# First stage of a fused cross-attention and feed-forward kernel: context loads one chunk ahead of x's, q's tanh one step later, a fourth PSUM bank

## The chip, the core and the metric

The kernel runs on one core of a Trainium2 chip. The metric is the device time of one execution in microseconds (us). Before the change it is 258.02 us, the median of three runs (257.67 to 258.16).

## The reference

The inputs `x` and `ctx_1024` are 128 x 64 x 128 in f32: 8192 rows of D = 128 features, in 128 batches of 64 rows. What is computed, cut to what matters:

```
q = layernorm(x)                      # no gain or bias
k = v = ctx
prob(t) = clip(p / (sum(p) + 1e-8), 1e-8), p = tanh(t)*0.499 + 0.5
sid  = (prob(q) - prob(k)) @ (log prob(q) - log prob(k)).T     # per batch, 64 x 64
attn = softmax(-sid / sqrt(D))
f    = (v - attn @ v) @ W_diff.T + b_diff + q
out  = layernorm(gelu(layernorm(f) @ W1.T + b1) @ W2.T + b2 + f)
x    = x + out
y    = x + (fp8(layernorm(x)) @ fp8(Wf).T + bf)
```

## The kernel before, in words

The 8192 rows are 64 tiles of 128 rows, taken in 16 chunks of G = 4 tiles. A chunk of x or of the context is 128 x 512 in f32, 256 KB. The kernel has three stages, each written as a step function that `run_steps` calls with a growing step number; `at(lag)` gives the chunk that entered `lag` steps ago. Each engine (SP for loads, POOL, ACT, DVE, PE) has its own program with its own order of work, and the engines meet only at counting semaphores. Nothing reorders the work: the order written by hand is the order in which an engine does it.

The first stage, which the change touches, prepares all 16 chunks. For chunk k:

- SP, in `load` (L305): loads the context chunk into one of two buffers `ctx_c` (L309), as soon as the tanh of the chunk two before it has ended and PE has transposed that chunk; then x's chunk (L312), once DVE has the variance of the chunk two before (L311). The waits hold up everything that is behind them on SP. Between the loads stand those of W1 (L316), W2 and small rows.
- ACT, in `phase1` (L520): at lag 0 four tanh of k, each with a sum (L525), and the copy of the transposed context out of PSUM (`vT_c`, L530); at lag 1 the copy of the product with W_diff out of PSUM (`PV`, L536); at lag 2 four tanh of q (L541). Once, eight steps in, it scales W1 (`W1h`, L547).
- PE, in `phase1` (L986): at lag 0 four transposes of the context (L992), at lag 1 four products with W_diff into one of three banks `P_B` (L1001), at lag 2 the bias row added by a matmul with a selector (L1010). The bank of chunk k is free when DVE has added the product of chunk k-3 (L999). At the step of `W_AT` = 6 it turns W1 and multiplies W2 (L1015, L1016).
- DVE, in `phase1` (L791): at lag 0 the statistics of x (L796) and, later in the step, the variance (L753 to L768); at lag 3 the sum of the product in PSUM and q into `F` (L801), which waits for q's tanh; at lag 1 the normalised q (L822), after POOL's power (L365). Two steps also copy the products of W1 and W2 (L804, L806), and one splits W1 (L810).
- After step 13 of lag 3, `take_norms` (L770, L777 to L787) turns the sums of 14 chunks into the gains that the second stage needs, and after the last step those of the last two chunks. Then the second stage begins, on DVE with L852.

The second stage (`phase2`) makes the differences and log ratios, the similarities, the softmax and the product with v. The third (`phase3`) runs the MLP, the two layer norms, the fp8 product and the stores.

Of the kernel before, what the change touches and what calls it, by code (L numbers as in the profile page):

```python
# [37 lines left out]
def wait(eng, sem, count):  # L38

    if count <= 0:  # L40
        return
    eng.wait_ge(sem, count)


def is_piece(k, n):

    return k.live and k.n == n
# [8 lines left out]
def xattn_ffn_kernel(nc, x, ctx_in, W_diff, b_diff, ln_g, ln_b, W1, b1, W2, b2, Wf, bf, out):  # L56
# [32 lines left out]
    out_d = out.rearrange("b s d -> (b s) d").rearrange("(t p) d -> p t d", p=P)  # L89

    EARLY = 2
    NORMS = NC - 2
    BF_HERE = NP - 3
    XQ_HERE = NP - 4
# [2 lines left out]
    with ExitStack() as ctx:  # L97
# [86 lines left out]
        centre = E_c[:, D:2 * D]  # L184
        sel_raw = E_c[:, 2 * D:3 * D]

        VT_B, P_B = (bank[0], bank[7]), (bank[1], bank[2], bank[6])
        D_B, L_B, S_B, EP_B = bank[2], bank[3], (bank[4], bank[7]), (bank[5], bank[6], bank[1])
        M1_B, M2_B, HT_B, XQ_B, FF_B = (bank[2], bank[3], bank[7]), (bank[4], bank[1]), bank[0], bank[5], bank[6]

# [111 lines left out]

        @block.sync
        def _(sp):
            def load(k):  # L305

                wait(sp, tanh_k, k.n - 1)
                wait(sp, vT_ps, k.n - 1)
                sp.dma_start(tiles(buf(ctx_c, k)), ctx_d[:, k.at:k.at + k.g]).then_inc(ctx_sem[k.buf], 16)  # L309

                wait(sp, x_var, k.n - 1)  # L311
                sp.dma_start(tiles(chunk(X, k)), x_d[:, k.at:k.at + k.g]).then_inc(x_in[k.buf], 16)  # L312

            for k in chunks[0:5]:
                load(k)
            sp.dma_start(W1_raw.rearrange("p (j d) -> p j d", d=D),  # L316
                         W1.rearrange("(j p) d -> p j d", p=P)).then_inc(w_in, 16)
            load(chunks[5])
            sp.dma_start(W2_raw, W2).then_inc(w_in, 16)
            load(chunks[6])  # L320
            sp.dma_start(g_col[:, :], ln_g.unsqueeze(1), allow_slow_non_contiguous=True).then_inc(w_in, 16)
            sp.dma_start(b_col[:, :], ln_b.unsqueeze(1), allow_slow_non_contiguous=True).then_inc(w_in, 16)
            sp.dma_start(b1_raw[:, :], b1.rearrange("(j p) -> p j", p=P),
                         allow_slow_non_contiguous=True).then_inc(w_in, 16)
            for k in chunks[7:]:
                load(k)
            for row, vec in ((b2_r, b2), (g_r, ln_g), (bf_r, bf)):
                sp.dma_start(row, vec.unsqueeze(0).broadcast_to([P, D])).then_inc(rows_in, 16)
            sp.wait_ge(bd_hl_ready, 1)
            sp.dma_start(Wf_raw, Wf).then_inc(wf_in, 16)  # L330

            def phase3(at):
                for k in last_of(at):
                    sp.wait_ge(y_ready, k.n + 1)
                    sp.dma_start(out_d[:, k.at:k.at + k.g], tiles(chunk(F, k))).then_inc(stored, 16)
                k = at(3)
                if k.live and k.n < XQ_HERE:
                    sp.wait_ge(xq16_ready, k.n + 1)
                    wait(sp, ff_ps, k.n - 1)
                    sp.dma_start_transpose(tiles(buf(xqT_c, k)), buf(xq16_c, k)).then_inc(xqT_in[k.buf], 16)  # L340

            run_steps(pieces, 4, phase3)
            sp.wait_ge(stored, 16 * NP)
# [168 lines left out]
        def _(act):  # L512
# [7 lines left out]
            def phase1(at):  # L520
                k = at(0)
                if k.live:
                    act.wait_ge(ctx_sem[k.buf], 16 * (k.n // 2 + 1))
                    for i in range(k.g):
                        last = act.activation(all_tile(TK, k, i), tile(ctx_c, k, i), ACT.Tanh,  # L525
                                              accum_out=per_tile(SUMK, k, i))
                    last.then_inc(tanh_k, 1)
                    act.wait_ge(vT_ps, k.n + 1)
                    wait(act, P_ps, k.n - 1)
                    act.activation(buf(vT_c, k), VT_B[k.buf][:, 0:k.g * D], ACT.Copy).then_inc(vT_sb, 1)  # L530
                k = at(1)
                if k.live:
                    act.wait_ge(P_ps, k.n + 1)
                    if is_piece(k, 0):
                        act.wait_ge(consts, CONSTS)
                    act.activation(pv_chunk(k), tiles(P_B[k.n % 3][:, 0:k.g * D]), ACT.Copy).then_inc(P_sb, 1)  # L536
                k = at(2)
                if k.live:
                    act.wait_ge(q_ready, k.n + 1)
                    for i in range(k.g):  # L540
                        last = act.activation(all_tile(TQ, k, i), all_tile(F, k, i), ACT.Tanh,  # L541
                                              accum_out=per_tile(SUMQ, k, i))
                    last.then_inc(tanh_q, 1)
                if is_piece(k, W_AT + 2):
                    act.wait_ge(w1u_sb, 1)
                    act.wait_ge(w_in, 16 * 5)
                    act.activation(W1h[:, :], W1u, ACT.Identity, scale=g_col[:, 0:1]).then_inc(w_sb, 1)  # L547

            run_steps(chunks, 2, phase1)

            act.preload_act_table_set("natural_log_exp_and_others")

# [163 lines left out]
        def _(dve):  # L716
# [72 lines left out]
                dve.wait_ge(norms, part + 1)  # L789

            def phase1(at):  # L791
                s, q, r = at(0), at(1), at(3)
                if s.live:
                    dve.wait_ge(x_in[s.buf], 16 * (s.n // 2 + 1))
                    for i in range(s.g):
                        last = dve.bn_stats(xstat[:, (s.buf * G + i) * 6:(s.buf * G + i + 1) * 6], all_tile(X, s, i))  # L796
                    last.then_inc(x_bn, 1)
                if r.live:
                    dve.wait_ge(tanh_q, r.n + 1)
                    dve.wait_ge(pb_ps, r.n + 1)  # L800
                    dve.tensor_tensor(chunk(F, r), P_B[r.n % 3][:, 0:r.g * D], chunk(F, r), ALU.add).then_inc(pq_ready, 1)  # L801
                if is_piece(r, W_AT):
                    dve.wait_ge(w_ps, 1)
                    dve.tensor_copy(W1u, bank[3][:, :]).then_inc(w1u_sb, 1)  # L804
                if is_piece(r, W_AT + 1):
                    dve.tensor_copy(W2T[:, :], bank[4][:, :]).then_inc(wt_sb, 1)  # L806
                if is_piece(q, NC - 1):

                    dve.wait_ge(w_sb, 1)
                    dve.scalar_tensor_tensor(out=W1l[:, :], in0=bank[3][:, :], scalar=g_col[:, 0:1],  # L810
                                             in1=W1h[:, :].bitcast(F32), op0=ALU.mult,
                                             op1=ALU.subtract).then_inc(w_done, 1)
                if s.live:
                    wait(dve, q_ready, s.n - 1)
                    stats_terms(s, x_bn, x_halves)
                    stats_halves(s, x_halves, x_terms)
                    stats_var(s, x_terms, x_var)
                if q.live:
                    dve.wait_ge(x_rstd, q.n + 1)
                    for i in range(q.g):  # L820
                        m = (q.buf * G + i) * 2
                        last = dve.tensor_scalar(all_tile(F, q, i), all_tile(X, q, i), xmv[:, m:m + 1],  # L822
                                                 xrstd[:, q.buf * G + i:q.buf * G + i + 1], ALU.subtract, ALU.mult)
                    last.then_inc(q_ready, 1)
                if is_piece(r, NORMS - 1):
                    take_norms(0, NORMS, 0)

                    dve.wait_ge(b1_ps, 1)
                    dve.tensor_tensor(b1c[:, :], bank[5][:, 0:HB], b1_raw[:, :], ALU.add).then_inc(b1_ready, 1)

            run_steps(chunks, 3, phase1)

            take_norms(NORMS, NC, 1)

# [145 lines left out]
        def _(pe):  # L980
# [5 lines left out]
            def phase1(at):  # L986
# [8 lines left out]
                if k.live:  # L995
                    if is_piece(k, 0):
                        pe.wait_ge(wd_sb, 1)
                    pe.wait_ge(vT_sb, k.n + 1)
                    wait(pe, pq_ready, k.n - 2)  # L999
                    for i in range(k.g):  # L1000
                        last = pe.matmul(P_B[k.n % 3][:, i * D:(i + 1) * D], tile(vT_c, k, i), WdT[:, :],  # L1001
                                         start=(i == 0), stop=False, skip_group_check=True)
                    last.then_inc(P_ps, 1)
                k = at(2)
                if k.live:
                    if is_piece(k, 0):
                        pe.wait_ge(bd_hl_ready, 1)
                        pe.wait_ge(sel_ready, 1)
                    pe.wait_ge(P_sb, k.n + 1)
                    pe.matmul(P_B[k.n % 3][:, 0:k.g * D], sel[:, :], over_tiles(bd_hl[:, :], k.g), start=False, stop=True,  # L1010
                              skip_group_check=True).then_inc(pb_ps, 1)
                if is_piece(k, W_AT):
                    pe.wait_ge(w_in, 16 * 5)
# [8 lines left out]

            pe.wait_ge(wt_sb, 1)
            for j in range(HB):
                last = pe.matmul(bank[5][:, j:j + 1], W1u[:, j * D:(j + 1) * D], b_col[:, :], start=True, stop=True)
            last.then_inc(b1_ps, 1)

            def turn_h(h):
# [148 lines left out]
```

## Time and profile before

| what | value |
|---|---|
| median of 3 runs | 258.02 us (257.67 to 258.16) |
| the profiled execution's own time | 258.79 us |
| its span in the profile | 256.9 us |
| busy: PE, DVE, ACT, POOL | 208.1, 222.6, 217.6, 190.3 us |
| first stage, to the start of its last `take_norms` | 64.5 us |
| mean granted TensorE clock | 0.937 of full |

The span is the time between the first and the last instruction that the profile shows; the execution's own time is 1.89 us more. Busy times say how full an engine was over the whole kernel, not which one set the end. For that the chain of waits is followed, and for a stage the timeline, where each instruction has its start, its duration and, in brackets, how long its engine had been idle and what released it.

### The profile page before, as it was taken

Reading aid. Unit: us, or ns where it says so; the run is one execution under the profiler, and the core shown is the slowest. Engines: PE = TensorE matmul, PEld = TensorE weight load, DVE = VectorE, ACT = ScalarE, POOL = GpSimd, SP = SyncE. Lnnn points to the kernel's source line nnn. Section 1 sums busy time; section 2 is a strip of 40 time slices with the busy share of each in tenths; the row PEclk is TensorE's granted clock in tenths of the full one; section 3 lists DMA queues with packets and bytes.
Section 4 is the critical chain, followed back from the end, with each engine's and each line's share of the span. In section 5 each row is a group of like instructions: output and inputs, shape, how many; then the busy total and the mean of one; then the engine's idle time right before and its main releaser. Section 6 shows DMA issues by size and latency. Waiting matters only on the chain.

```text
span 256.9 us, 5935 instructions
## 1 busy us (share of the span) xinstructions
PE 208.1 (81%) x1727; PEld 177.8 (69%) x1727; DVE 222.6 (87%) x835; ACT 217.6 (85%) x782; POOL 190.3 (74%) x253
## 2 busy tenths in 40 slices
PE   2678695655399888986899999999999999998621
PEld 1656584434287666665699999889999999888610
DVE  1999999998879999999633889999999999999983
ACT  4499999998889999988997889988888777876672
POOL 2477656765799999992878496969869698666773
PEclk9997889997569999999999999999999999999955
DMA  5677554540000000000307388698878999987614
GB/s 130 193 218 197 163 153 134 158 125 0 3 0 3 0 3 3 1 3 4 41 0 88 37 106 104 112 149 130 125 124 124 144 113 133 136 130 113 100 41 124
DMA packets 50816, 23.52 MB, mean 92 GB/s; under 512 B 9312, under 2 KB 50656, under 8 KB 50784
## 3 DMA queue, kind: packets, MB, share of 16 engines
q0 software_dynamic: 15856, 7.87, 27.5%
q1 hardware_dynamic: 34496, 15.08, 21.7%
q10 hardware_dynamic: 432, 0.20, 0.4%
q8 instruction: 14, 0.23, 0.4%
q14 instruction: 18, 0.15, 0.2%
HBM read 9.37 MB, written 4.19 MB: 53 GB/s over the span
## 4 chain that ended last, share of the span: by engine, by line
POOL 27%; DVE 24%; ACT 21%; issue 13%; PE 10%; DMA 3%; SPq 0%; POOLq 0%; DVEq 0%; ACTq 0%
POOL F L410 8%; ACT TQK L525 6%; POOL xrstd L452 6%; ACT TQK L541 6%; DVE LN_c L860 5%; POOL orstd L445 5%; DVE q_c L852 5%; POOL F L466 5%; DVE F L880 5%; PE bank L1052 3%; DMA LN_c<-in_ctx_dram 3%; ACT PV L536 3%; ACT vT_c L530 3%; DVE F L905 1%; POOL HALFK L478 1%
## 5 line engine op out<-in xcount | busy, mean ns | idle before, releaser
L1052 PEld LDWEIGHTS bank<-W2T,TQK 128*128 128x128 f32 x512 | 62.9, 191 | 4.6 <-ACT TQK L563 1.2
L1052 PE MATMUL bank<-W2T,TQK 128*128 128x128 f32 x512 | 64.5, 277 | 1.1 <-ACT TQK L563 1.1
L563 ACT ACTIVATE TQK<-bank,b1c 128x512 f32<-128x512 f32 (+1 forms) x68 | 42.9, 664 | 4.6 <-PE bank L1045 4.1
L452 POOL TENSOR_TENSOR xrstd<-xvar,pow_c 128x4 f32<-128x4 f32 (+1 forms) x17 | 18.2, 1072 | 20.4 <-DVE xvar L768 20.4
L365 POOL TENSOR_TENSOR xrstd<-xvar,pow_c 128x4 f32<-128x4 f32 x16 | 16.8, 1052 | 21.2 <-DVE xvar L768 21.2
L1043 PE MATMUL bank<-hTh,W1h 128*128 128x512 f32 (+1 forms) x68 | 30.0, 442 | 0.8 <-DVE hTl L843 0.8
L410 POOL DMA_DIRECT2D F<-rows x17 | 26.0, 1529 | 5.2 <-DVE E_c L838 5.2
L1044 PE MATMUL bank<-hTl,W1h 128*128 128x512 f32 (+1 forms) x68 | 26.0, 382 | 0.0
L1045 PE MATMUL bank<-hTh,W1l 128*128 128x512 f32 (+1 forms) x68 | 25.9, 381 | 0.0
L1001 PE MATMUL bank<-WdT,vT_c 128*128 128x128 f32 x128 | 21.8, 324 | 4.1 <-ACT vT_c L530 3.7
L1001 PEld LDWEIGHTS bank<-WdT,vT_c 128*128 128x128 f32 x128 | 19.3, 231 | 6.5 <-ACT vT_c L530 6.5
L992 PE MATMUL bank<-ident,LN_c 128*128 128x128 f32 x64 | 12.6, 330 | 13.5 <-DMA LN_c<-in_ctx_dram 13.4
L371 POOL TENSOR_TENSOR X<-X,rows 128x512 f32<-128x512 f32 x16 | 20.3, 1269 | 2.0 <-DVE F L822 2.0
L525 ACT ACTIVATE TQK<-LN_c 128x128 f32<-128x128 f32 x64 | 19.2, 325 | 2.4 <-DMA LN_c<-in_ctx_dram 2.4
L992 PEld LDWEIGHTS bank<-ident,LN_c 128*128 128x128 f32 x64 | 8.6, 166 | 17.5 <-DMA LN_c<-in_ctx_dram 17.3
L466 POOL DMA_DIRECT2D F<-rows x14 | 18.6, 1326 | 2.8 <-issue 2.8
L648 ACT ACTIVATE TQK<-F 128x128 f32<-128x128 f32 x64 | 19.0, 314 | 1.2 <-DVE F L900 1.2
L681 ACT ACTIVATE LN_c<-LN_c 128x512 bf16<-128x512 fp8e4 x13 | 8.2, 631 | 13.8 <-DVE LN_c L925 13.8
L1070 PE MATMUL bank<-PV,E_c 64*64 64x129 f32 x256 | 18.4, 282 | 1.6 <-ACT E_c L597 1.6
L860 DVE SCALAR_TENSOR_TENSOR LN_c<-LN_c,LRATIO 128x128 f32<-128x128 f32 x49 | 19.7, 453 | 0.0
L541 ACT ACTIVATE TQK<-F 128x128 f32<-128x128 f32 x64 | 19.3, 330 | 0.2 <-DVE F L822 0.2
L568 ACT ACTIVATE TQK<-F 128x128 f32<-128x128 f32 x64 | 19.0, 312 | 0.0
(131 smaller groups left out, 655.9 us busy)
## 6 DMA issues: line engine op xcount, KB each, us to landing
F<-rows POOLq DMA_DIRECT2D x29, 256.0 KB, 4.7
LN_c<-in_ctx_dram SPq DMA_DIRECT2D x16, 256.0 KB, 3.0
X<-in_x_dram SPq DMA_DIRECT2D x16, 256.0 KB, 3.3
out_dram<-F SPq DMA_DIRECT2D x15, 256.0 KB, 2.4
LN_c<-in_L_xattn_W_dram SPq DMA_DIRECT2D x1, 256.0 KB, 3.9
lT_c<-in_L_xattn_W_dram SPq DMA_DIRECT2D x1, 256.0 KB, 3.7
F<-rows POOLq DMA_DIRECT2D x2, 128.0 KB, 4.8
out_dram<-F SPq DMA_DIRECT2D x2, 128.0 KB, 1.8
```

What stands on the lines that cost most here:

```text
L410: pool.dma_start(tiles(chunk(F, k)), over_tiles(b2_r, k.g), accum_op=ALU.add).then_inc(b2_added[k.n % 3], 16)
L452: pool.tensor_tensor(buf(xrstd, x1, G), buf(xvar, x1, G), pow_c[:, 0:x1.g], ALU.pow).then_inc(x1_rstd, 1)
L466: pool.dma_start(tiles(chunk(F, x1)), over_tiles(bf_r, x1.g), accum_op=ALU.add).then_inc(bf_added[x1.n % 3], 16)
L525: last = act.activation(all_tile(TK, k, i), tile(ctx_c, k, i), ACT.Tanh, accum_out=per_tile(SUMK, k, i))
L541: last = act.activation(all_tile(TQ, k, i), all_tile(F, k, i), ACT.Tanh, accum_out=per_tile(SUMQ, k, i))
L563: act.activation(hid(m, j), m1_bank(m, j), ACT.Gelu, bias=b1c[:, j:j + 1]).then_inc(gelu_ready, 1)
L860: last = dve.scalar_tensor_tensor(out=ln_tile(1, k, i), in0=ln_tile(0, k, i), scalar=per_tile(LRATIO, k, i), in1=ln_tile(1, k, i), op0=ALU ...
L1001: last = pe.matmul(P_B[k.n % 3][:, i * D:(i + 1) * D], tile(vT_c, k, i), WdT[:, :], start=(i == 0), stop=False, skip_group_check=True)
L1043: pe.matmul(ps, w_hi, buf(hTh, m), start=True, stop=False)
L1044: pe.matmul(ps, w_hi, buf(hTl, m), start=False, stop=False)
L1045: pe.matmul(ps, w_lo, buf(hTh, m), start=False, stop=True).then_inc(m1_ps, 1)
L1052: last = pe.matmul(M2_B[m.buf][:, i * D:(i + 1) * D], hid(m, j)[:, i * D:(i + 1) * D], W2T[:, j * D:(j + 1) * D], start=(j == 0 and i == 0 ...
```

## The change

The context's loads are issued one chunk ahead of x's (`CTX_LEAD = 1`): context 0, context 1, x 0, context 2, x 1, and so on. Their waits stay those they were, for the same chunk. ACT takes q's tanh at lag 3 instead of lag 2, and DVE's sum with the product moves from lag 3 to lag 4 with it, so that both loops have one step more. The products with W_diff rotate over four banks instead of three: `bank[5]` is added, and b1's product moves from `bank[5]` to `bank[4]`. The wait in PE's loop looks one chunk further back. The scaling of W1 on ACT stays in the same step of ACT's loop (lag 3 of chunk 7 instead of lag 2 of chunk 8); the copies of W1's and W2's products on DVE, tied to lag 4, come one step later.

```diff
+    CTX_LEAD = 1
...
-        VT_B, P_B = (bank[0], bank[7]), (bank[1], bank[2], bank[6])
+        VT_B, P_B = (bank[0], bank[7]), (bank[1], bank[2], bank[6], bank[5])
...
         @block.sync
-            def load(k):
-
+            def load_ctx(k):
                 wait(sp, tanh_k, k.n - 1)
                 wait(sp, vT_ps, k.n - 1)
                 sp.dma_start(tiles(buf(ctx_c, k)), ctx_d[:, k.at:k.at + k.g]).then_inc(ctx_sem[k.buf], 16)
 
+            def load(k):
+                if k.n + CTX_LEAD < NC:
+                    load_ctx(chunks[k.n + CTX_LEAD])
                 wait(sp, x_var, k.n - 1)
                 sp.dma_start(tiles(chunk(X, k)), x_d[:, k.at:k.at + k.g]).then_inc(x_in[k.buf], 16)
 
+            for k in chunks[0:CTX_LEAD]:
+                load_ctx(k)
             for k in chunks[0:5]:
                 load(k)
...
         ACT, phase1
-                    act.activation(pv_chunk(k), tiles(P_B[k.n % 3][:, 0:k.g * D]), ACT.Copy).then_inc(P_sb, 1)
-                k = at(2)
+                    act.activation(pv_chunk(k), tiles(P_B[k.n % 4][:, 0:k.g * D]), ACT.Copy).then_inc(P_sb, 1)
+                k = at(3)
                 if k.live:
                     act.wait_ge(q_ready, k.n + 1)
...
-                if is_piece(k, W_AT + 2):
+                if is_piece(k, W_AT + 1):
                     act.wait_ge(w1u_sb, 1)
...
-            run_steps(chunks, 2, phase1)
+            run_steps(chunks, 3, phase1)
...
         DVE, phase1
-                s, q, r = at(0), at(1), at(3)
+                s, q, r = at(0), at(1), at(4)
...
-                    dve.tensor_tensor(chunk(F, r), P_B[r.n % 3][:, 0:r.g * D], chunk(F, r), ALU.add).then_inc(pq_ready, 1)
+                    dve.tensor_tensor(chunk(F, r), P_B[r.n % 4][:, 0:r.g * D], chunk(F, r), ALU.add).then_inc(pq_ready, 1)
...
-                    dve.tensor_tensor(b1c[:, :], bank[5][:, 0:HB], b1_raw[:, :], ALU.add).then_inc(b1_ready, 1)
-
-            run_steps(chunks, 3, phase1)
+                    dve.tensor_tensor(b1c[:, :], bank[4][:, 0:HB], b1_raw[:, :], ALU.add).then_inc(b1_ready, 1)
+
+            run_steps(chunks, 4, phase1)
...
         PE, phase1
-                    wait(pe, pq_ready, k.n - 2)
+                    wait(pe, pq_ready, k.n - 3)
                     for i in range(k.g):
-                        last = pe.matmul(P_B[k.n % 3][:, i * D:(i + 1) * D], tile(vT_c, k, i), WdT[:, :],
+                        last = pe.matmul(P_B[k.n % 4][:, i * D:(i + 1) * D], tile(vT_c, k, i), WdT[:, :],
...
-                    pe.matmul(P_B[k.n % 3][:, 0:k.g * D], sel[:, :], over_tiles(bd_hl[:, :], k.g), start=False, stop=True,
+                    pe.matmul(P_B[k.n % 4][:, 0:k.g * D], sel[:, :], over_tiles(bd_hl[:, :], k.g), start=False, stop=True,
...
-                last = pe.matmul(bank[5][:, j:j + 1], W1u[:, j * D:(j + 1) * D], b_col[:, :], start=True, stop=True)
+                last = pe.matmul(bank[4][:, j:j + 1], W1u[:, j * D:(j + 1) * D], b_col[:, :], start=True, stop=True)
```

## Rows read from the trace of the kernel before

**Rows 1.** The page: busy times, TensorE clock in 40 slices, and the chain's shares.
```profile
PE 208.1 (81%) x1727; PEld 177.8 (69%) x1727; DVE 222.6 (87%) x835; ACT 217.6 (85%) x782; POOL 190.3 (74%) x253
...
PEclk9997889997569999999999999999999999999955
...
POOL 27%; DVE 24%; ACT 21%; issue 13%; PE 10%; DMA 3%; SPq 0%; POOLq 0%; DVEq 0%; ACTq 0%
```

**Rows 2.** Waits, 0 to 70 us: who waited for whom, us in total, times, longest.
```profile
ACT TQK L525 <- DMA LN_c<-in_ctx_dram: 2.4, 1, 2.4
...
DVE F L801 <- ACT TQK L541: 0.9, 1, 0.9
```

**Rows 3.** Timeline of the start: start us, duration us, engine, line, instruction, [idle before].
```profile
1.24 0.49 SPq L312 DMA_DIRECT2D X<-in_x_dram  x1
1.78 0.50 SPq L309 DMA_DIRECT2D LN_c<-in_ctx_dram  x1
...
5.76 0.37 SPq L309 DMA_DIRECT2D LN_c<-in_ctx_dram  x1
...
7.66 0.87 DVE L796 BATCH_NORM_STATS2 xstat<-X 128x6 f32<-128x128 f32 x4
...
8.65 1.12 PE L992 MATMUL bank<-ident,LN_c 128*128 128x128 f32 x4 [3.42 <-DMA LN_c<-in_ctx_dram]
...
12.01 0.30 ACT L525 ACTIVATE TQK<-LN_c 128x128 f32<-128x128 f32 x1
```

**Rows 4.** DMA to landing: x 0; line L309 (contexts, 0 to 70 us); L312 (x).
```profile
X<-in_x_dram SPq DMA_DIRECT2D x1, 256.0 KB, 6.3
...
DMA to landing us min/median/max: 2.6/3.0/6.8
...
DMA to landing us min/median/max: 2.8/3.3/7.1
```

**Rows 5.** Timeline, DVE: the statistics of two chunks that follow each other.
```profile
18.15 0.86 DVE L796 BATCH_NORM_STATS2 xstat<-X 128x6 f32<-128x128 f32 x4
...
21.23 0.86 DVE L796 BATCH_NORM_STATS2 xstat<-X 128x6 f32<-128x128 f32 x4
```

**Rows 6.** Timeline of the steady part, late in the first stage.
```profile
46.94 0.37 SPq L309 DMA_DIRECT2D LN_c<-in_ctx_dram  x1
...
50.24 0.37 SPq L309 DMA_DIRECT2D LN_c<-in_ctx_dram  x1
...
50.65 0.51 SPq L312 DMA_DIRECT2D X<-in_x_dram  x1
50.74 1.16 PE L1001 MATMUL bank<-WdT,vT_c 128*128 128x128 f32 x8 [0.34 <-ACT vT_c L530]
...
54.70 0.86 DVE L796 BATCH_NORM_STATS2 xstat<-X 128x6 f32<-128x128 f32 x4
...
55.67 0.69 DVE L801 TENSOR_TENSOR F<-bank,F 128x512 f32<-128x512 f32 x1
```

**Rows 7.** Windows (busy by engine, then clock, DMA), and the timeline of that stretch.
```profile
20.00:22.00 2.00, 2.00 (x11) 1.94 (x10) 1.97 (x11) 2.00 (x11) 1.63 (x2) 0.50 0.62 203
...
20.57 1.94 PE L1001 MATMUL bank<-WdT,vT_c 128*128 128x128 f32 x8
```

**Rows 8.** Chain in order of time (start, us, what), and DVE's copy of W1's product.
```profile
41.83 0.61 ACT W1h L547
...
49.04 1.17 ACT TQK L525 x8
50.21 0.48 ACT vT_c L530
...
35.87 0.68 DVE L804 COPY LN_c<-bank 128x512 f32<-128x512 f32 x1
```

**Rows 9.** Timeline, DVE: the last gains of the first stage begin.
```profile
64.50 0.17 DVE L777 TENSOR_SCALAR NORM<-SUM 128x16 f32<-128x16 f32 x1
```

**Rows 10.** Windows of 10 us in the second stage: width, busy time by engine, clock, DMA.
```profile
80.00:90.00 10.00, 8.69 (x124) 6.64 (x122) 9.89 (x36) 9.47 (x19) 9.21 (x19) 1.00 0.00 0
```

## The prediction

> **What bounds the kernel now.** I read the page first, for the engines and the chain, then the waits of the first 70 us, then the timeline of the start, of one steady chunk and of the end of the first stage. In the page no engine is idle enough to be out of the question, and the chain that ended last is spread over POOL, DVE and ACT [rows 1]: it changes hands by stage, so the change is to be judged in the first stage alone. In the waits the reader is to see how little ACT and DVE wait there: ACT 2.4 us once for the second context, DVE 0.9 us once, for q's tanh at the end [rows 2]. A steady chunk costs ACT 3.30 us: four tanh of k 1.17, copy of vT 0.48 [rows 8], the copy of PV and the four tanh of q, of the same sizes, which is also the distance between two context loads (46.94 to 50.24) [rows 6]. DVE alone needs 3.08 us per chunk (18.15 to 21.23, before it had caught up with ACT) [rows 5]. So ACT sets the pace, and DVE has only 0.22 us per chunk in hand. In the second stage DVE is busy 9.89 of 10 us [rows 10], so whatever time the last gains of the first stage begin (64.50 now [rows 9]) goes through to the end unchanged; that start is the quantity that I work out.
>
> **The change part by part.**
>
> Call T(n) the moment at which the four tanh of k of chunk n are done; T(13) is 50.21 [rows 8].
>
> *Start of ACT, a gain.* Context 1 now takes the place of x 0 in the queue: issued at 1.24, it lands after x 0's 6.3 us at 7.5, where it landed at 1.78 + 6.8 = 8.6 before [rows 3, 4] (6.8 is the longest of the contexts). The transposes, the product and the copies behind it keep their distance (8.65 to the next tanh at 12.01 [rows 3]), so chunk 2's tanh starts at 10.9 instead of 12.01: 1.1 us earlier. In the step that follows ACT no longer takes q's tanh of chunk 0, 1.17 us, which goes to the end of the stage. So ACT is 1.1 + 1.17 = 2.3 us ahead from chunk 3 on; its total work is the same.
>
> *Loads of x, the other side.* x 0 takes context 1's place and lands at 8.6 instead of 7.5. What matters more is the steady part. SP issues in order, and x(n) now stands behind context(n+1), whose wait is for the tanh of chunk n-1. Before, it stood behind context(n), released one chunk earlier. In the trace context 15 is issued at 50.24, 0.03 after T(13), x 15 at 50.65, 0.44 after T(13) [rows 6, 8], and an x takes 3.3 us to land, its median [rows 4]. In the new order x(n) lands at T(n-1) + 0.44 + 3.3 = T(n-1) + 3.74, and DVE's statistics cannot start before that. Statistics 15 began at 54.70 [rows 6], which is T(14) + 1.19 (T(14) = 50.21 + 3.30): each x comes 2.5 us later against ACT than DVE took it. q's tanh has gained 3.30 us of lag, so ACT does not wait for it; DVE, which has the last word, does.
>
> A rule of the Trainium skill (DMA: Bandwidth & Descriptors, Anatomy of one DMA) puts a transfer at about 2.0 us plus its bytes at 436 GB/s, which for 256 KB would be an estimate of 2.6 us; the trace has 3.3 us for x [rows 4], and the page's fit is for the GpSimd's path. By 2.6 us the sum below would be 0.7 us lower; the row decides.
>
> *Fourth bank.* P(n) waits for DVE's sum of chunk n-4. In a DVE step that sum ends 0.97 - 0.22 + 0.69 = 1.44 us after the statistics begin (54.70 to 55.67, less the wait for ACT that a step of 3.30 holds over one of 3.08) [rows 5, 6], so at T(n-1) + 3.74 + 1.44 = T(n) + 1.88. Then 1.16 us for the product [rows 6]: T(n) + 3.1. ACT wants it for its copy after the tanh and the vT copy of the next chunk, at 3.30 + 0.48 = 3.8, or 0.16 sooner since its instructions overlap. So at the full clock 0.5 us is left and ACT doesn't wait. With three banks the product would wait for the sum of the next chunk, 3.30 later; the fourth bank is what lets the late x pass, no gain in itself.
>
> *TensorE at its lower level.* Around 20 to 22 us the granted clock is 0.50, the 1.2 GHz level, and the product takes 1.94 us instead of 1.16 [rows 6, 7]. Before, that had 2 us of cover, since the product started right behind vT. Now the product would end at T(n) + 1.9 + 1.94 = 3.85, some 0.25 us late for ACT, and with slower transposes and bias matmul around it up to 0.7. As x's loads hang on ACT, and DVE hangs on x, what is lost is not caught up. On the page the clock is down in the fourth to sixth slices, 19 to 39 us [rows 1]. Bounds: 0 if none falls under a product that matters, 1.4 us for two at 0.7. I take one half, 0.7.
>
> *W1 and W2.* PE's block for them stands ahead of a product that now has only 0.5 us of slack: up to 0.3 us late. DVE copies W1's product one step later (sum at +1.44, copy 0.68 [rows 8]), in T(10)'s frame at 3.74 + 1.44 + 0.68 - 3.30 = 2.56; ACT comes to its scaling at 1.17 + 0.48 + 0.48 = 2.13: a wait of 0.4 at most, less what PE's block has already cost. Together 0 to 0.7, I take 0.5. The scaling itself (0.61 [rows 8]) is in the same step. b1's other bank, the constants and the `% 4` cost nothing: they lie between waits of PE and DVE that others set.
>
> *The sum.* T(13) after = 50.21 - 2.3 + 0.5 = 48.4. x 14 lands at 48.4 + 3.74 = 52.15. x 15 has no context ahead of it and is not late, so DVE takes it one step of 3.08 later: 55.2, against 54.70, 0.5 us later. From there to the last gains were 64.50 - 54.70 = 9.80 us [rows 6, 9]. DVE's wait of 0.9 for q's tanh [rows 2] and the 0.22 of its step go, as ACT is ahead; one sum more (0.66 of the row's 0.69) falls into this tail, since the lag is four: 9.80 - 0.9 - 0.22 + 0.66 = 9.34. The gains begin at 64.6, 0.1 later than before; with 0.7 for the clock 65.3, 0.8 later. So the span goes from 256.9 to 257.7 and the profiled execution from 258.79 to 259.6; that execution is 0.77 above the median of the runs, and put on the median of 258.02 the forecast is 258.8 us.
>
> **The rivals.**
>
> *Rival 1, faster: the start is worth more than I allow and DVE is not gated.* Nothing shows that context 1 must wait as long as x 0 did. A context takes 3.0 us at the median [rows 4]; at 1.24 + 3.0 = 4.2 context 1 would be there before ACT is free, 0.48 after the tanh that released the load at 5.76 [rows 3], so at 6.2. Chunk 2's tanh then starts 3.36 later at 9.6 (context 2, 5.76 + 3.0, is there), and ACT is 2.4 + 1.17 = 3.6 us ahead, 1.3 more than above. x at the short end of its landings, 2.8 us [rows 4], gives 0.5 more. With the base of +0.1 that is -1.7 at most; DVE, which starts later, can hardly follow all of it, and I take -0.7: 257.3 us. It decides if the x loads stay under 3 us or context 1 lands by 6.5. Against it: x 0 took 6.3 us in that place, with the first small loads beside it. The Trainium skill (DMA: Bandwidth & Descriptors, Rules for kernel authors) says to issue a load early and wait for it late; by that rule the context's lead is a gain, which is this rival. The trace bears it out only for context 1: later contexts are held by the same tanh as before.
>
> *Rival 2, no change.* The 2.3 us ahead and the 2.5 us behind cancel, and no low clock falls under a product: 64.6, so 258.1 us. For it: the base sum is within 0.2 of before. Against it: the low stretches were there twice and the cover is gone.
>
> *Rival 3, much slower: the loop of ACT, SP and DVE locks to TensorE at 1.2 GHz.* If the idle gap that PE gets ahead of each product (from its transposes to T(n) + 1.9) brings the lower level more often, five or six chunks lose 0.25 to 0.7 us each, say 2 us over the base: 260.1 us. It decides from the point at which more than two chunks in the stage have products of 1.9 us and ACT waits before its PV copy.
>
> **How the numbers follow.** The forecast (+0.8) has 0.38, rival 1 0.27, rival 2 0.20, rival 3 0.15. About 0.2%, 0.5 us, is what a measurement can tell from none. The forecast's own spread of 0.3 to 1.4 puts 0.05 of it below the bound: faster 0.27, same 0.25, slower 0.48. The range reaches to rival 1's middle and past rival 3's: 257.1 to 260.4; the forecast's own is 258.3 to 259.4.
>
> **What would show each step.** Context 1's tanh at 7.5 instead of 8.63, chunk 3's 2.3 us earlier than before, no q tanh in the third step. In the steady part SP's x load right behind a context that waited for ACT's tanh, DVE waiting at L796 for x by DMA instead of at L801 for ACT, and the product L1001 released by DVE's L801 rather than ACT's vT. A wait of ACT at W1h of some 0.4 us. Waits of ACT at L536 in chunks where the product takes 1.9 us. The last `take_norms` at 65.3. I am wrong if DVE's statistics are not released by x's DMA, if the last gains begin before 64.0, or if the second and third stages are not simply shifted.

## The result: 0.42% slower, and the profile after

Over 14 runs of each, the changed kernel takes 259.5 us (258.7 to 261.13) and the kernel before 258.49 us (257.5 to 259.49); the ratio is 1.0042, 95% interval 1.0025 to 1.0058, so about 1.1 us slower. The profiled execution took 259.15 us, its span is 257.3 us. Of all the executions behind this document one was in the chip's slow state (265.8 us at a mean clock of 0.818, of the version with the early lead and POOL's addition moved), and the ratios leave it out.

First the page of the changed kernel: busy times, TensorE's clock in 40 slices, the shares of the chain that ended last.

```profile
PE 205.4 (80%) x1727; PEld 176.8 (69%) x1727; DVE 223.0 (87%) x835; ACT 217.7 (85%) x782; POOL 189.9 (74%) x253
...
PEclk9999999985559999999999999999999999999975
...
DVE 29%; POOL 27%; issue 15%; PE 11%; ACT 9%; DMA 6%; SPq 1%; POOLq 0%; DVEq 0%; ACTq 0%
```

The work of the engines is that of [rows 1] within 0.4 us (PE apart, whose clock was full in the middle of the first stage here). The chain has changed hands: ACT has gone from 21% to 9%, DVE and DMA have taken it. The waits of the first 70 us say where:

```profile
ACT PV L541 <- PE bank L1006: 2.9, 2, 1.8
...
ACT TQK L530 <- DMA LN_c<-in_ctx_dram: 0.5, 1, 0.5
ACT W1h L552 <- DVE LN_c L809: 0.3, 1, 0.3
...
DVE xstat L801 <- DMA X<-in_x_dram: 2.2, 6, 0.9
...
PE bank L1006 <- DVE F L806: 18.2, 12, 2.4
```

ACT's wait for the second context has shrunk from 2.4 [rows 2] to 0.5 us. DVE no longer waits for q's tanh, but in six of the sixteen chunks for x. And PE waits 18.2 us for DVE's sum before the product, twelve times; before, the product was released by ACT's copy of the transposed context (the bracket of L1001 in [rows 6]). The start, in the timeline (start, duration, engine, line, instruction, idle before):

```profile
6.76 0.31 ACT L530 ACTIVATE TQK<-LN_c 128x128 f32<-128x128 f32 x1 [0.49 <-DMA LN_c<-in_ctx_dram]
...
7.69 0.87 DVE L801 BATCH_NORM_STATS2 xstat<-X 128x6 f32<-128x128 f32 x4 [0.94 <-DMA X<-in_x_dram]
...
10.13 0.30 ACT L530 ACTIVATE TQK<-LN_c 128x128 f32<-128x128 f32 x1
...
12.49 0.30 ACT L530 ACTIVATE TQK<-LN_c 128x128 f32<-128x128 f32 x1
```

Chunk 2's tanh starts at 10.13 against 12.01 [rows 3]. Chunk 3's starts at 12.49, and in the trace of the kernel before it is this line:

```profile
15.34 0.30 ACT L525 ACTIVATE TQK<-LN_c 128x128 f32<-128x128 f32 x1
```

So ACT is 2.85 us ahead. One turn of the loop that then sets the pace, from the chain in order of time (start, duration, what):

```profile
15.88 1.18 ACT TQK L530 x8
17.08 0.37 SPq L309
17.45 0.04 issue
17.49 4.00 DMA X<-in_x_dram
21.49 0.03 issue
21.52 0.04 DVE xstat L801
...
21.73 0.66 DVE xstat L801 x3
22.39 0.60 DVE F L806
22.99 0.14 issue
23.12 1.14 PE bank L1006 x8
24.27 0.02 issue
24.29 0.60 ACT PV L541
```

The whole loop of the forecast is in it: the tanh of chunk 4 lets SP issue context 6 at 17.08, x 5 goes right behind it and lands 4.00 us later, DVE starts on it at once, its sum (of chunk 1) frees the bank, and only then come the product and ACT's copy. The end of the stage, in the timeline:

```profile
60.38 0.69 DVE L806 TENSOR_TENSOR F<-bank,F 128x512 f32<-128x512 f32 x1
60.44 1.26 POOL L376 TENSOR_TENSOR X<-X,rows 128x512 f32<-128x512 f32 x1 [1.01 <-DVE F L827]
60.99 0.79 DVE L782 TENSOR_SCALAR NORM<-SUM 128x112 f32<-128x112 f32 x1
...
64.66 0.17 DVE L782 TENSOR_SCALAR NORM<-SUM 128x16 f32<-128x16 f32 x1
```

The last gains begin at 64.66, against 64.50 [rows 9]: of the 1.1 us, this execution shows only 0.16 in the first stage. The spans of the two profiled executions differ by 0.4 us. The experiments had to say what the rest is, and what the parts of the change are worth.

### The profile page after: what moved, and what is told of

It is laid out like the page before. It is cut to its first block, busy times and chain, and to the rows that moved or that the text cites. A ratio compares the mean times of both kernels' runs of the same rounds, so it can differ in the third digit from the quotient of the medians.

```text
span 257.3 us, 5934 instructions
## 1 busy us (share of the span) xinstructions
PE 205.4 (80%) x1727; PEld 176.8 (69%) x1727; DVE 223.0 (87%) x835; ACT 217.7 (85%) x782; POOL 189.9 (74%) x253
## 4 chain that ended last, share of the span: by engine, by line
DVE 29%; POOL 27%; issue 15%; PE 11%; ACT 9%; DMA 6%; SPq 1%; POOLq 0%; DVEq 0%; ACTq 0%
POOL F L415 8%; POOL xrstd L457 6%; POOL orstd L450 5%; DVE q_c L857 5%; DVE LN_c L865 5%; DVE F L885 5%; POOL F L471 5%; DMA X<-in_x_dram 4%; ACT TQK L530 3%; PE bank L1057 3%; DMA LN_c<-in_ctx_dram 2%; DVE F L827 2%; ACT TQK L546 2%; DVE xstat L801 2%; PE bank L1006 2%
## 5 line engine op out<-in xcount | busy, mean ns | idle before, releaser
L1057 PE MATMUL bank<-W2T,TQK 128*128 128x128 f32 x512 | 64.6, 277 | 1.1 <-ACT TQK L568 1.1
L1006 PE MATMUL bank<-WdT,vT_c 128*128 128x128 f32 x128 | 20.2, 308 | 18.2 <-DVE F L806 18.2
L457 POOL TENSOR_TENSOR xrstd<-xvar,pow_c 128x4 f32<-128x4 f32 (+1 forms) x17 | 18.2, 1069 | 20.5 <-DVE xvar L773 20.5
L1006 PEld LDWEIGHTS bank<-WdT,vT_c 128*128 128x128 f32 x128 | 17.9, 217 | 20.7 <-issue 18.6
L857 DVE SCALAR_TENSOR_TENSOR q_c<-TQK,GAINQ,q_c 128x128 f32<-128x128 f32 x49 | 17.8, 413 | 2.0 <-POOL q_c L388 2.0
L865 DVE SCALAR_TENSOR_TENSOR LN_c<-LN_c,LRATIO 128x128 f32<-128x128 f32 x49 | 18.8, 435 | 0.0
L885 DVE SCALAR_TENSOR_TENSOR F<-bank,nrden,F 128x128 f32<-128x128 f32 x64 | 18.1, 345 | 0.6
```

The costliest lines, as they stand in the source:

```text
L457: pool.tensor_tensor(buf(xrstd, x1, G), buf(xvar, x1, G), pow_c[:, 0:x1.g], ALU.pow).then_inc(x1_rstd, 1)
L857: last = dve.scalar_tensor_tensor(out=tile(diff_c, k, i), in0=all_tile(TQ, k, i), scalar=per_tile(GAINQ, k, i), in1=tile(diff_c, k, i), op ...
L865: last = dve.scalar_tensor_tensor(out=ln_tile(1, k, i), in0=ln_tile(0, k, i), scalar=per_tile(LRATIO, k, i), in1=ln_tile(1, k, i), op0=ALU ...
L885: last = dve.scalar_tensor_tensor(out=all_tile(F, k, i), in0=ep, scalar=nrden[:, k.buf * G + i:k.buf * G + i + 1], in1=all_tile(F, k, i), ...
L1006: last = pe.matmul(P_B[k.n % 4][:, i * D:(i + 1) * D], tile(vT_c, k, i), WdT[:, :], start=(i == 0), stop=False, skip_group_check=True)
L1057: last = pe.matmul(M2_B[m.buf][:, i * D:(i + 1) * D], hid(m, j)[:, i * D:(i + 1) * D], W2T[:, j * D:(j + 1) * D], start=(j == 0 and i == 0 ...
```

## The experiments

Ratios are those of each kernel against the kernel before, run beside it on the same chip. The runs fall into sets: the changed kernel's own; the four versions of the table below; the three on POOL's addition and the early lead; and the two with transposes. The medians of the kernel before in them are 258.49, 258.98, 259.28 and 258.93 us, so a step of some tenths of a per cent is surer inside a set than between two. "Last gains" is the start of the last `take_norms` on DVE, the quantity that the prediction works out.

### Parts of the change, one by one

Four kernels make a table of load order against lag. **Lag alone** is the changed kernel with `CTX_LEAD = 0`:

```diff
-    CTX_LEAD = 1
+    CTX_LEAD = 0
```

> The changed kernel with the loads in the old order (context k, x k); q's tanh at lag 3 and four banks stay. Theory 1 (x behind the next context holds DVE back): DVE no longer waits for x at its statistics in the steady part, the product is no longer released late by DVE's sum of four chunks before with only 0.5 us to spare, and the last gains begin at 64.2 to 64.7, against 64.50 before and 64.66 after: -0.3 to +0.2 us against before, so 0.5 to 1.3 us faster than the changed kernel. Context 1's tanh is back at 8.6, and ACT is ahead of before by one q tanh (1.17 us) alone. Theory 2 (the lag itself costs, by the sum that falls into DVE's tail): the time stays that of the changed kernel, +1.1 us against before. Theory 3 (TensorE's low clock makes the difference): nothing is gained in a run whose clock is full in the stage.

Measured: 0.9992 (0.9974 to 1.0011), last gains 64.31. DVE did not wait for x in the steady part (0.3 us once, at the start).

```profile
64.31 0.16 DVE L782 TENSOR_SCALAR NORM<-SUM 128x16 f32<-128x16 f32 x1
```

**Lead alone** is the kernel before with the changed `load`, lag 2 and three banks:

```diff
+            def load_ctx(k): ...
             def load(k):
+                if k.n + CTX_LEAD < NC:
+                    load_ctx(chunks[k.n + CTX_LEAD])
                 wait(sp, x_var, k.n - 1)
                 sp.dma_start(tiles(chunk(X, k)), ...)
...
+            for k in chunks[0:CTX_LEAD]:
+                load_ctx(k)
```

> The kernel before with the context one chunk ahead of x's, q's tanh still at lag 2 and three banks. Theory 1: x lands at T(n-1) + 3.74 and DVE waits for it at its statistics as in the changed kernel; the last gains begin at 64.5 to 65.9, 0 to 1.3 us after those before, as with the changed kernel (+1.1 us) or a little worse, since q's normalised chunk now comes late for ACT's tanh at the end. Theory 2 (the lag costs): the time is that of before or better by the start, -1 us. Chunk 2's tanh starts at 10.1 as in the changed kernel in either case.

Measured: 1.0003 (0.9980 to 1.0025), last gains 64.64. PE waited 17.6 us for DVE's sum before the product, as in the changed kernel.

```profile
PE bank L1006 <- DVE F L806: 17.6, 12, 2.0
...
64.64 0.16 DVE L782 TENSOR_SCALAR NORM<-SUM 128x16 f32<-128x16 f32 x1
```

**Context 1 ahead, and no other**, with the lag of three and with the old lag:

```diff
             def load(k):
+                if k.n > 1:
+                    load_ctx(k)
                 wait(sp, x_var, k.n - 1)
...
+            for k in chunks[0:2]:
+                load_ctx(k)
```

> The changed kernel, but only context 1 goes ahead (context 0, context 1, x 0, x 1, context 2, x 2, context 3, ...): from chunk 2 on each x stands behind its own context as before. Theory 1: the start's gain stays (chunk 2's tanh at 10.1 or 10.4), DVE is not held by x in the steady part and runs at its own 3.08 us per chunk; statistics of chunk 15 at 52.9 to 53.5 instead of 54.90, last gains at 63.0 to 63.5: 1.0 to 1.8 us faster than before, 1.5 to 3 us faster than the changed kernel. Theory 2 or 3 (lag, or clock, and not the place of x): no faster than before by more than 0.3 us.

> The kernel before with nothing changed but the first loads: context 0, context 1, x 0, x 1, then context k, x k; q's tanh at lag 2, three banks. Theory 1: ACT is 1.9 us ahead from chunk 2 on, DVE follows at 3.08 us per chunk since its wait for q's tanh goes; last gains at 63.0 to 63.7, 0.8 to 1.7 us faster than before. If it is as fast as the same with lag 3, the lag and the fourth bank bring nothing. Theory 2 (the lag costs): 0.7 us faster than the version with lag 3. Rival: DVE is the bound already, so an earlier context brings nothing, 0 +- 0.3 us.

Measured: 0.9986 (0.9969 to 1.0004) with last gains 64.26 at lag 3; 0.9936 (0.9915 to 0.9957), 1.65 us faster than before, with last gains 63.46 at lag 2. Its statistics of chunk 15 and its gains:

```profile
54.03 0.86 DVE L800 BATCH_NORM_STATS2 xstat<-X 128x6 f32<-128x128 f32 x4
...
63.46 0.17 DVE L781 TENSOR_SCALAR NORM<-SUM 128x16 f32<-128x16 f32 x1
```

| loads | lag 2 | lag 3 |
|---|---|---|
| order of before | 1 | 0.9992 |
| context 1 ahead only | 0.9936 | 0.9986 |
| every context ahead | 1.0003 | 1.0042 |

Two things follow. Going down from the second row to the third costs 0.6% at either lag: theory 1 (x behind the next context) holds, 1.7 us at lag 2 and 1.4 us at lag 3. Going right costs nothing in the first row, where ACT is the bound, and 0.4 to 0.5% in the others: theory 2 holds too, which I had meant as its rival. Past the first chunks both parts of the change cost, and what pays for them is the one load at the start. The steps to the changed kernel (1.0042) are steps between two sets of runs; those inside one set, 0.9936 to 1.0003 and 0.9936 to 0.9986, carry the argument without them. In the third row the traces do not show the cost of the lag directly, 64.64 against 64.66: the execution at lag 2 has a low stretch of TensorE's clock from 44 to 52 us (0.75 and 0.50), over which one chunk's step of ACT takes 3.71 us instead of 3.29, and the one at lag 3 has none there.

The version with lag 3 fell short of its expectation of 1.0 to 1.8 us, and its trace shows a second wait in the queue:

```profile
10.11 0.37 SPq L315 DMA_DIRECT2D X<-in_x_dram  x1
...
10.58 0.45 SPq L309 DMA_DIRECT2D LN_c<-in_ctx_dram  x1
...
13.95 0.31 ACT L530 ACTIVATE TQK<-LN_c 128x128 f32<-128x128 f32 x1 [1.00 <-DMA LN_c<-in_ctx_dram]
```

Context 3 stands behind x 2, which waits until 10.11 for the variance of chunk 0; chunk 3's tanh then starts at 13.95 instead of 12.49. The same queue blocks in the other direction. It is worth little here: once DVE has caught up it goes at its own 3.09 us per chunk, and in the end it waits only 0.24 us for ACT. The version at lag 2 has the same block (x 2 at 10.06) and is faster. What sets the two apart is the tail from the statistics of chunk 15 to the last gains, 10.09 us (54.17 to 64.26) against 9.43 (54.03 to 63.46), and that is the subject of the next section.

### Why the lag costs: POOL's last addition

In every lag-3 trace with POOL's addition in its place the first operation of the gains (128x112) takes 0.79 to 0.91 us, against 0.20 to 0.21 at lag 2.

```diff
-                if k.live:
-                    pool.wait_ge(q_ready, k.n + 1)
-                    ...
-                    pool.tensor_tensor(tiles(chunk(X, k)), tiles(chunk(X, k)), over_tiles(b_r, k.g), ...
+                if k.live and k.n < NC - 1:
+                    shift_x(k)
...
+            shift_x(chunks[NC - 1])
             pool.wait_ge(rows_ready, 1)
```

`shift_x` holds the addition as it was; its call for the last chunk now stands behind POOL's part of the second stage.

> The changed kernel, but POOL adds ln_b to the last chunk of x after its part of the second stage and not right behind DVE's last normalised q. Theory A (in the changed kernel the first operation of the last gains on DVE, 128x112, takes 0.79 us instead of 0.21 because it starts while POOL's 1.26 us addition runs and ends only with it): that operation takes 0.2 us again, the last gains begin at 64.1 instead of 64.66, and the kernel is 0.4 to 0.7 us faster than the changed one, so +0.4 to +0.7 us against before. Theory B (the 0.79 is a wait for ACT's sums): it stays 0.7 or more and nothing is gained, +1.1 us against before.

Measured: 1.0003 (0.9983 to 1.0023), and in its trace:

```profile
60.98 0.21 DVE L786 TENSOR_SCALAR NORM<-SUM 128x112 f32<-128x112 f32 x1
...
64.07 0.16 DVE L786 TENSOR_SCALAR NORM<-SUM 128x16 f32<-128x16 f32 x1
```

Theory A is shown: same start (60.98 for 60.99), 0.21 instead of 0.79, last gains 0.59 earlier. ACT's sums were there. At lag 3 DVE's sum of chunk 13 comes between the last normalised q and the gains, so that POOL's addition, which the last q releases, is already running when the gains begin. With the addition moved the tail is 9.17 us (54.90 to 64.07). So the lag costs the end of the stage two things, the extra sum of some 0.66 us and 0.59 us under the addition. How much the move is worth in time is less sure: 1.0003 against the 1.0042 of the changed kernel is again a step between two sets, and it is more (1.0 us) than the 0.59 that the stage shows.

### Keeping both starts

```diff
             def load(k):
+                if k.n < 4:
+                    load_ctx(chunks[k.n + 1])
+                elif k.n > 4:
+                    load_ctx(k)
                 wait(sp, x_var, k.n - 1)
...
+            load_ctx(chunks[0])
```

> The kernel before (lag 2, three banks) with the context one chunk ahead of x for chunks 0 to 3 alone; from chunk 5 on context k, x k. Theory 1: both starts are kept, x 0 at 7.7 on DVE (8.3 in the version where x 1 goes second) and context 1 at 6.8 on ACT; from chunk 4 on DVE is not held by x and goes at its own 3.09 us; statistics of chunk 15 at 53.3, last gains at 62.7 to 63.0: 1.5 to 2.2 us faster than before, 0 to 0.7 faster than the version with only context 1 ahead. Rival (ACT is the bound again in the steady part): statistics of chunk 15 at 54 or later, no faster than that version.

Measured: 0.9939 (0.9923 to 0.9954), last gains 63.22, statistics of chunk 15 at 53.58. x 0 was there at 7.61, as expected, and from chunk 4 on DVE went at 3.09 us (3.69 in the two steps with the copies of W1's and W2's products). In time it is the same as the version with context 1 alone; the 0.24 us that its trace gains in the stage is under what the runs tell.

> As the version with the lead for chunks 0 to 3 at lag 2, with POOL's last addition moved as well. At lag 2 only 0.15 us of a DVE operation (128x56, 0.34 instead of 0.19) lay under that addition, so theory A expects 0.1 to 0.2 us more gain and no more: 1.6 to 2.4 us faster than before. If it is slower, the addition costs POOL something where it stands now, in front of the third stage.

Measured: 0.9932 (0.9912 to 0.9952), last gains 62.77. It has the lowest ratio of all, 1.75 us under before, but its interval overlaps with those of the version above and of the one with context 1 alone, so that moving the addition at lag 2 is not shown to gain anything.

### The fourth bank

```diff
-                    wait(pe, pq_ready, k.n - 3)
+                    wait(pe, pq_ready, k.n - 2)
                     for i in range(k.g):
-                        last = pe.matmul(P_B[k.n % 4][:, i * D:(i + 1) * D], tile(vT_c, k, i), WdT[:, :],
+                        last = pe.matmul(P_B[k.n % 3][:, i * D:(i + 1) * D], tile(vT_c, k, i), WdT[:, :],
...
```

> The changed kernel with three banks instead of four for the product with W_diff. The prediction's step on the fourth bank: the product of chunk n then waits for DVE's sum of chunk n-3, which DVE makes one step later, after x of the next chunk has come, which waits for ACT's tanh, which waits for the copy of that product: the loop closes and each chunk costs some 1.1 us more, 13 to 18 us in all (272 to 276 us). If the fourth bank were a gain of its own and not a need of the new order, the loss would be 1 us or less.

Measured: 281.67 us, one run, 22 us over before, more than the 13 to 18 expected. Its waits in the first 90 us:

```profile
ACT PV L541 <- PE bank L1006: 24.2, 15, 4.2
DVE xstat L801 <- DMA X<-in_x_dram: 17.5, 11, 3.0
```

The loop closes as described: ACT waits for the product 15 times. The fourth bank is a need, no gain. It is needed for the new order of loads and the lag of three together: the new order with lag 2 runs on three banks at 1.0003. The clock was also lower in this stage (0.50 from 32 to 44 us, mean of the run 0.882), which the expectation had left out; how much of the excess is due to it was not tried.

### TensorE's clock

The first trace of the changed kernel has the full clock in the middle of the stage. A second one of each kernel:

> The changed kernel once more, for a second trace. If the late return of TensorE's clock in the second stage (third to fourth chunk 4.16 us) is a property of the order of the work, it is there again with the last gains at 64.6 to 64.8; if it is chance of one execution, the step is between 3.4 and 4.2 and the span moves with it. If low stretches of the clock fall into the middle of the first stage here, the last gains begin up to 1.4 us later.

> The kernel before once more. The last gains at 64.3 to 64.8, as ACT's pace sets them and low stretches of TensorE's clock are covered; the third-to-fourth step of the second stage 3.4 to 4.2 (3.80 in the first trace).

The changed kernel again took 260.78 us, span 259.0. Windows (width, busy by engine, clock, DMA) and timeline:

```profile
20.00:24.00 4.00, 3.66 (x16) 3.37 (x16) 3.86 (x23) 2.67 (x15) 2.48 (x3) 0.50 0.82 230
```

```profile
20.34 2.04 PE L1006 MATMUL bank<-WdT,vT_c 128*128 128x128 f32 x8 [2.65 <-DVE F L806]
...
22.42 0.60 ACT L541 ACTIVATE PV<-bank 128x512 f32<-128x512 f32 x1 [1.33 <-PE bank L1006]
...
66.13 0.17 DVE L782 TENSOR_SCALAR NORM<-SUM 128x16 f32<-128x16 f32 x1
```

One stretch at 0.50 (1.2 GHz), after PE had waited 2.65 us for DVE's sum: the product takes 2.04 us, ACT stands 1.33 us, and the last gains begin 1.47 us later than in the first trace. Most of that falls in this one place: from chunk 5's tanh to chunk 6's ACT takes 4.75 us, 3.44 in the first trace. In the kernel before, again (259.34 us, span 257.5):

```profile
44.00:48.00 4.00, 3.60 (x14) 2.92 (x15) 3.90 (x21) 4.00 (x21) 2.81 (x3) 0.57 0.44 131
```

```profile
44.40 1.98 PE L1001 MATMUL bank<-WdT,vT_c 128*128 128x128 f32 x8 [0.74 <-ACT vT_c L530]
...
64.75 0.17 DVE L777 TENSOR_SCALAR NORM<-SUM 128x16 f32<-128x16 f32 x1
```

The same slow product, ACT busy 4.00 of 4 us beside it, and gains at 64.75: covered, as in [rows 7]. So in the first stage the changed kernel is 0.2 us behind in the execution without a low stretch under a product in the middle of it, and 1.4 us in the one with it. The trace of the changed kernel with transposes, below, has the same order of work in this stage and is a third case, with a product of 2.03 us in the same place and the same last gains:

```profile
21.94 0.60 ACT L542 ACTIVATE PV<-bank 128x512 f32<-128x512 f32 x1 [1.24 <-PE bank L1007]
...
66.13 0.17 DVE L783 TENSOR_SCALAR NORM<-SUM 128x16 f32<-128x16 f32 x1
```

That this is what makes up the 1.1 us of the timed runs is not shown. The span goes with the mean clock in the 14 runs of the changed kernel (the three at 0.918 have 258.2, 258.9 and 259.3 us, the five at 0.939 and 0.940 have 257.2 to 257.7, but one at 0.933 has 259.2), and it does so in the kernel before as well: of its 67 runs beside the experiments the 17 at 0.945 or more have 255.9 to 257.2, the 29 at 0.932 or less 256.7 to 258.4. And if the runs of the changed kernel were a mixture of +0.2 and +1.4, the fastest of each kernel would lie 0.2 apart; they lie 1.2 apart (258.70 and 257.50).

The last pair tests the second stage, with 20 transposes of the identity into a bank that nobody reads, in PE's gap between the stages:

```diff
             last.then_inc(b1_ps, 1)
+            for j in range(20):
+                pe.transpose(bank[0][:, (j % 4) * D:(j % 4 + 1) * D], ident[:, :], ident[:, :])
```

> The changed kernel with 20 transposes of the identity on TensorE, whose results nothing reads, between the first and the second stage, where it is otherwise idle for 5 to 6 us. Theory W (the second stage is not simply shifted: in the changed kernel TensorE is at 0.50 until past 76 us and DVE's fourth chunk of the stage comes 4.16 us after the third, instead of 3.4): with TensorE active in the gap the clock is back before 72 us, the third-to-fourth step is 3.4 to 3.5 us and the first steps are shorter too, 0.7 to 1.5 us faster than the changed kernel, so -0.4 to +0.4 us against before. Rival: the first chunks of the stage are paced by DVE at either clock and nothing changes, or the transposes run past DVE's first chunk and cost up to 1 us.

> The version with the lead for chunks 0 to 3, lag 2 and POOL's last addition moved, with the same 20 transposes in the gap. Theory W: the step from third to fourth chunk falls from 3.62 to 3.4, the earlier ones a little, 0.2 to 1.0 us faster than without them, 2.0 to 3.0 us faster than before. Rival: nothing, since this version's clock is already back in 72 to 76 us (0.89 there).

Measured: 1.0070 (1.0042 to 1.0099) on the changed kernel and 0.9942 (0.9918 to 0.9966) on the other: no gain shown, though the step that theory W names did what it said. DVE's third and fourth chunk of the second stage in the changed kernel, and with the transposes:

```profile
72.70 0.91 DVE L857 SCALAR_TENSOR_TENSOR q_c<-TQK,GAINQ,q_c 128x128 f32<-128x128 f32 x3 [1.34 <-POOL q_c L388]
76.86 1.19 DVE L857 SCALAR_TENSOR_TENSOR q_c<-TQK,GAINQ,q_c 128x128 f32<-128x128 f32 x3
```

```profile
74.19 0.91 DVE L858 SCALAR_TENSOR_TENSOR q_c<-TQK,GAINQ,q_c 128x128 f32<-128x128 f32 x3 [1.35 <-POOL q_c L389]
77.62 0.91 DVE L858 SCALAR_TENSOR_TENSOR q_c<-TQK,GAINQ,q_c 128x128 f32<-128x128 f32 x3
```

4.16 us became 3.43. But that execution had low stretches in the first stage (last gains 66.13), and over the runs the step's 0.7 us does not show. The trace that compares best, the second one of the changed kernel, with the same last gains of 66.13 and of the same set, has a span of 259.0 us against 258.1 here. But the changed kernel was not timed beside the warmed one beyond that single run. Theory W is right about the step; its gain in time is not shown, and why stays open.

## Why the prediction was right, step by step

It forecast +0.8 us; +1.1 was measured. The mechanism (x behind the next context, DVE held by x, the product held by DVE) is shown by the chain, by the table and by the bank. The size is right in part by luck: two errors cancel in the stage, and the term for the clock is not confirmed.

- **Start of ACT**: forecast 2.3 us ahead, measured 2.85. The landing was mis-sized: context 1 came at 6.7 and not at 7.5, and x 0 at 7.7 and not at 8.6, since x 1 is no longer in the queue with them; where it is (context 1 ahead only), x 0 came at 8.34. This is the half of rival 1 that came true.
- **x's landing**: forecast T(n-1) + 3.74. For chunk 14, T(13) is 48.10, x was issued at 48.52 and DVE began at 51.80, T(13) + 3.70. Right.
- **W1's scaling**: forecast a wait of ACT up to 0.4, measured 0.3. The step with the scaling took ACT 4.40 us, 3.91 before: 0.49, against the 0.5 forecast. It lost 0.30 more where the forecast had nothing at the full clock: two steps, of chunks 5 to 6 and 6 to 7, took 3.44 instead of 3.29, the second behind the x that needed 4.00 us to land. So 0.5 us of slack at the product was too much. T(13) came at 48.10 all the same, 0.3 sooner than the forecast 48.4, by the better start.
- **The tail**: forecast 9.34 us from the statistics of chunk 15 to the last gains, measured 64.66 - 54.90 = 9.76, against 9.80 before. This step failed: I counted the extra sum (0.66) and not that it pushes the first operation of the gains under POOL's addition (0.58); with that moved, the tail was 9.17. The earlier start cancelled it, which is luck: 64.66 measured, 64.6 forecast for the full clock.
- **Clock**: 0 to 1.4 forecast, 0.7 taken, which puts the last gains at 65.3. No trace has that: the two show 64.66 and 66.13, a term of 0 and of 1.47. Their spans are 0.4 and 1.5 us over those of the kernel before, the mean of which is near the measured 1.1 us, but two pairs do not show that it is made up so, and the fastest runs, 1.2 us apart, speak against it. What the 1.1 us is beyond the 0.16 of the first trace stays open.
- **The later stages as a plain shift**: not quite, which the prediction had named as a sign of being wrong. DVE's last chunk of the second stage comes 0.34 us after that of before where its first came 0.17 after; the step of 4.16 us is 3.80 before. In the second traces that step is 4.13 and 4.05.
- **The fourth bank as a need**: right. **Rival 2** (the sums cancel) is what the first stage of the first trace looks like, but not the time: the fastest of the 14 runs took 258.70 us, over rival 2's 258.1. **Rival 3** has the mechanism of the second trace, with one stretch instead of five.

## What to carry to other kernels

When loads of two streams share an in-order queue, look at what each wait holds up for the other stream: a load moved ahead brings nothing if its own wait stays, and the stream behind it inherits that wait. Count the slack of the engine that ends the stage, not of the one that sets its pace: here 0.22 us per chunk on DVE. A reordering that costs almost nothing in a trace at the full clock (0.16 us here) can still turn covered slow stretches of TensorE into lost time (1.47 us later in the next trace), so take more than one trace; and at the end of a stage a longer lag puts work into the tail and shifts what runs beside what.

## What the runs showed of the hardware

- A DVE operation with a 128x112 input and output took 0.21 us alone and 0.79 to 0.91 us when it began while POOL's 1.26 us addition ran, ending with it (60.99 + 0.79 = 61.78; 60.44 + 1.26 = 61.70). DVE's sum from PSUM beside the same addition took its usual 0.69 us. The Trainium skill (SBUF — State Buffer, Who interferes with whom) has the rule: a `tensor_scalar` can take the port pair that DVE and GpSimd share, the one that starts first holds it for its whole instruction, and the other blocks. The traces agree.
- The granted clock is not a property of the kernel alone: the changed kernel kept 1.00 from 20 to 24 us in one execution and had 0.50 in another, after waits of PE for the same sum of 2.43 and 2.65 us.
- The second stage has more than one rhythm: with the same work of DVE there, the distance between DVE's chunks was 3.44 in the changed kernel and 3.41 with lag alone or POOL's addition moved, which over the chunks of the stage, with the fourth step, made 1.0 to 1.2 us. The slower rhythm goes with a long fourth step: where that step took 3.42 or 3.43 us (lag alone, POOL's addition moved in the changed kernel, both versions with transposes) the later distance was 3.41 to 3.42, and where it took 3.62 to 4.16 it was 3.44 to 3.47. What ties the two was not found.
